# Narrow attention in a sixteen-stage kernel: other loads, other places for the bf16 splits, and the division by token

## The reference

```python
q, k, v = proj(Wq, bq), proj(Wk, bk), proj(Wv, bv)      # [b, 16, n, 8]
score = jax.nn.softmax(jnp.einsum('bhif,bhjf->bhij', q, k) / SCALE, axis=-1)   # SCALE = 128 / 19.5
attn = jnp.einsum('bhij,bhjf->bihf', score, v)
o = attn.reshape(b, n, f) @ Wo.T + bo
x = x + o
```

## Time and profile before

| | |
|---|---|
| median of 3 executions | 3803.88 us (3800.67, 3803.88, 3805.98) |
| the profiled execution | 3797.76 us, span of its profile 3796.1 us, 33099 instructions |
| TensorE busy | 2777.9 us (73%) |
| VectorE busy | 1910.9 us (50%) |
| ScalarE busy | 1454.2 us (38%) |
| GpSimd busy | 563.0 us (15%) |
| mean granted TensorE clock | 0.872 |
| L0b, first and second trip | 270.1 to 467.4, 2155.0 to 2351.7 us |
| L2b, first and second trip | 1168.5 to 1343.3, 3053.0 to 3227.5 us |

### The profile page before, as it was taken

The page is one execution under the profiler, slowest core; times in us unless marked ns, Lnnn a source line. Parts: engine busy times, 40 slices in busy tenths (PEclk is TensorE's granted clock), DMA queues, the critical chain, the costliest instruction groups (busy, mean ns, idle before and its releaser), DMA issues. The chain is left out here.

```text
span 3796.1 us, 33099 instructions
## 1 busy us (share of the span) xinstructions
PE 2777.9 (73%) x11584; PEld 1230.2 (32%) x11630; DVE 1910.9 (50%) x2675; ACT 1454.2 (38%) x2370; POOL 563.0 (15%) x376
## 2 busy tenths in 40 slices
PE   3565778999695797573846567889996957965647
PEld 1221164544342343131212212635443423422312
DVE  4858642554315613872549575425533166148635
ACT  2442412654242444432434334036542423434323
POOL 0532000000014010430006400000000140105300
PEclk8897969999797998895969889599997979988969
DMA  2001000000011110002000020000000011100010
GB/s 85 0 1 42 10 1 1 1 1 1 6 39 30 23 45 0 0 3 20 1 12 0 0 44 8 1 1 1 1 1 28 17 34 18 45 0 0 9 14 6
DMA packets 103312, 52.11 MB, mean 14 GB/s; under 512 B 75232, under 2 KB 91616, under 8 KB 103136
## 3 DMA queue, kind: packets, MB, share of 16 engines
q1 hardware_dynamic: 103136, 49.88, 5.6%
HBM read 40.02 MB, written 9.44 MB: 13 GB/s over the span
## 5 line engine op out<-in xcount | busy, mean ns | idle before, releaser
L1598 ACT ACTIVATE L1b_pr<-ps,L1b_mneg 128x512 f32<-128x512 f32 x256 | 173.5, 683 | 196.1 <-DVE L1b_mneg L1637 196.1
L518 POOL TENSOR_TENSOR xs<-xs,L2f_part 128x512 f32<-128x512 f32 x32 | 40.5, 1265 | 1286.6 <-DVE L2f_part L507 1286.6
L1635 DVE TENSOR_REDUCE L1b_m<-ps 128x2 f32<-128x1024 f32 x128 | 156.8, 1225 | 104.9 <-PE ps L1502 100.8
L1356 ACT ACTIVATE L0b_pt<-ps 128x1024 f32<-128x1024 f32 x128 | 129.5, 1023 | 208.6 <-PE ps L1294 206.7
L90 ACT ACT_TABLE_LOAD x32 | 41.1, 1283 | 423.3 <-PEq L671 180.5
L1403 DVE TENSOR_REDUCE L0b_mx<-ps 128x1 f32<-128x512 f32 x256 | 161.3, 685 | 46.8 <-PE ps L1278 38.9
L1046 POOL TENSOR_TENSOR L0a_db<-L0a_du,L0a_bs 128x1024 f32<-128x1024 f32 x64 | 150.3, 2353 | 224.4 <-ACT L0a_bs L1017 213.7
L1046 POOL TENSOR_TENSOR L3a_db<-L3a_du,L3a_bs 128x1024 f32<-128x1024 f32 x64 | 150.3, 2352 | 224.6 <-ACT L3a_bs L1017 214.1
L1356 ACT ACTIVATE L2b_pt<-ps 128x1024 f32<-128x1024 f32 (+3 forms) x128 | 88.5, 703 | 204.8 <-PE ps L1297 204.3
L1278 PE MATMUL ps<-L0b_ks,L0b_qs 128*128 128x512 bf16 x246 | 100.7, 446 | 87.8 <-DMA L0b_ks<-parts_dram 51.9
L1661 DVE COPY L1b_prt<-ps 128x512 f32<-128x512 f32 x128 | 88.6, 692 | 124.8 <-PE ps L1513 124.5
(11 more groups left out here) (567 smaller groups left out, 5787.8 us busy)
## 6 DMA issues: line engine op xcount, KB each, us to landing
L2f_w<-expert_dram SPq DMA_DIRECT2D x32, 256.0 KB, 3.0
L2g_w<-expert_dram SPq DMA_DIRECT2D x32, 256.0 KB, 3.1
weights<-w_dram SPq DMA_DIRECT2D x7, 789.5 KB, 8.8
parts_dram<-L0b_cut SPq DMA_DIRECT2D x4, 768.0 KB, 3.3
L0b_qs<-parts_dram SPq DMA_DIRECT2D x96, 32.0 KB
L0b_ks<-parts_dram SPq DMA_DIRECT2D x96, 32.0 KB
parts_dram<-L2b_cut SPq DMA_DIRECT2D x4, 768.0 KB, 3.3
L2b_qs<-parts_dram SPq DMA_DIRECT2D x96, 32.0 KB
```

The source lines that it names most:

```text
L1356: act.activation(pt[:, n % 3, 2 * half:2 * half + 2, q0:T], g.ps[:, 2 * (s % 2):2 * (s % 2) + 2, q0:T], ACT.Exp).then_inc(prob, 1)
L1598: act.activation(pr[:, s % 2, h, :], g.ps[:, 2 * (s % 2) + h, :], ACT.Exp, bias=mneg[:, s % 2, h:h + 1], accum_out=total[:, u % 2, t, h:h ...
L1635: dve.tensor_reduce(m[:, s % 2, :], g.ps[:, 2 * (s % 2):2 * (s % 2) + 2, :], AX.X, ALU.max).then_inc(max_raw, 1)
```

## The change

- `qs` and `ks` have 50 rows rather than 128, the tops' matmuls run over 48 of them and the scores' over 50; the fills are gone, and the two rows of ones in `ks` come by one DMA. The maxima are cut in two parts, not three.
- Heads of a unit lie next to each other, so that a DMA can load several units. Each part is sent as soon as it is cut; unit 0 is loaded first, then the other three of batch 1 in twelve DMAs, then all of batch 2 in twelve.
- Batch 1 is projected when its own norm is done. VectorE cuts batch 1, GpSimd batch 2. GpSimd also makes the three steps of the maxima.
- LEAD is 28.
- The division: TensorE transposes the copied sums (`turn`, slots 19, 35, 51 and after the last), VectorE takes the reciprocal of 32 denominators per row and multiplies 256 sums by them, TensorE transposes back (`turn_back`, slots 22, 38, 54 and after the last), ScalarE adds the bias.
- Batch 1's output matmul stands in slot 41, its addition in slot 42.

(Removed code that the functions above show is mostly left out here.)

```diff
-    STACK = 16 * 2 * len(Q_PART)
-    AHEAD = 2
-    LEAD = 25
+    LEAD = 28
     UN = NB * 4
+    SLOTS = 8 * UN
+    PARTS = 3
+    LOADS = 16 * 2 * len(Q_PART)
...
-        qs = st.sb("qs", [P, NB, 4, 4, T], BF16)
-        ks = st.sb("ks", [P, NB, 4, 4, T], BF16)
-        cut = st.sb("cut", [P, 3, 2, T], BF16)
...
+        qs = st.sb("qs", [ROWS + 2, NB, H, T], BF16)
+        ks = st.sb("ks", [ROWS + 2, NB, H, T], BF16)
+        cut = st.sb("cut", [P, NB, PARTS, 2, T], BF16)
...
-                def send_parts(b):
...
-                def stack(u):
+                sp.dma_start(ks[ROWS:ROWS + 2, :, :, :].rearrange("p b h (r c) -> p (b h r) c", c=P),
+                             bcast(g.cb[0:2, 544:544 + P], 1, NB * H * KT)).then_inc(ones_in, 16)
+                def send(b, part):
+                    if b == 0:
+                        sp.wait_ge(cut_dve, part + 1)
+                    else:
+                        sp.wait_ge(cut_pool, part + 1)
+                    sp.dma_start(g.parts_dram[b, :, part, :, :], cut[:, b, part, :, :]).then_inc(sent[part], 16)
+                def load(b, i0, n, part, landed):
+                    sp.wait_ge(sent[part], 16 * (b + 1))
+                    for x, table, dst in ((0, Q_PART, qs), (1, K_PART, ks)):
+                        for j in range(len(table)):
+                            if table[j] == part:
+                                src = g.parts_dram[b, 32 * i0:32 * (i0 + n), part, x, :].rearrange("(h f) t -> f h t", f=DH)
+                                sp.dma_start(dst[DH * j:DH * j + DH, b, 4 * i0:4 * (i0 + n), :], src).then_inc(landed, 16)
+                def send_max(u):
                     b, i = u // 4, u % 4
...
-                    sp.wait_ge(stacked, STACK * (u + 1))
...
-                for u in range(AHEAD):
...
+                    for p, ready in enumerate((m_hi, m_lo)):
+                        sp.wait_ge(ready, u + 1)
+                        sp.dma_start(qs[ROWS + p:ROWS + p + 1, b, 4 * i:4 * i + 4, :].rearrange("o r (t c) -> o (r t) c", c=P),
                                      mcut[:, u % 2, p, :]).then_inc(m_rows, 16)
...
-                    if u + AHEAD < UN:
-                        stack(u + AHEAD)
+                    sp.wait_ge(m_rows, 32 * (u + 1))
+                send(0, 0)
+                send(0, 1)
+                load(0, 0, 1, 0, unit0_in)
+                send(0, 2)
+                load(0, 0, 1, 1, unit0_in)
+                load(0, 0, 1, 2, unit0_in)
+                for part in range(PARTS):
+                    load(0, 1, 3, part, first_in)
+                send_max(0)
+                for part in range(PARTS):
+                    send(1, part)
+                for part in range(PARTS):
+                    load(1, 0, 4, part, second_in)
+                for u in range(1, UN):
+                    send_max(u)
...
-                    pe.wait_ge(ln.done, NB)
...
+                    pe.wait_ge(ln.done, b + 1)
+                    qb, kb, vb = ((0, 1, 2), (3, 6, 7))[b]
+                    pe.matmul(g.ps[:, qb, :], g.w(w + "_wq"), g.xn[:, b, :], start=True, stop=True)
+                    pe.matmul(g.ps[:, kb, :], g.w(w + "_wk"), g.xn[:, b, :], start=True, stop=True).then_inc(proj, 1)
...
-                    mm = pe.matmul(g.ps[:, 4 + a % 2, 0:span(t)], qs[:, b, i, r, t * P:(t + 1) * P], ks[:, b, i, r, 0:span(t)],
+                        if u == 0:
+                            pe.wait_ge(unit0_in, LOADS)
+                        elif b == 0:
+                            pe.wait_ge(first_in, LOADS)
+                        else:
+                            pe.wait_ge(second_in, LOADS)
+                    h, t = 4 * i + n // 4, n % 4
+                    mm = pe.matmul(g.ps[:, 4 + a % 2, 0:span(t)], qs[0:ROWS, b, h, t * P:(t + 1) * P], ks[0:ROWS, b, h, 0:span(t)],
                                    start=True, stop=not causal)
...
-                        mm = pe.matmul(g.ps[:, bank, q0:T], ks[:, b, i, r, kt * P:(kt + 1) * P], qs[:, b, i, r, q0:T],
+                        h, bank = 4 * i + 2 * half + x, 2 * (s % 2) + x
+                        mm = pe.matmul(g.ps[:, bank, q0:T], ks[:, b, h, kt * P:(kt + 1) * P], qs[:, b, h, q0:T],
...
-                        mm = pe.matmul(g.ps[32 * r:32 * r + 32, 6 + i // 2, q0:T], vpad[:, b, kt, 4 * r + i, :], pt[:, n % 3, r, q0:T],
+                        mm = pe.matmul(g.ps[32 * r:32 * r + 32, 6 + i // 2, q0:T], vpad[:, b, kt, 4 * i + r, :], pt[:, n % 3, r, q0:T],
...
-                def spread_den(c):
+                def turn(c):
                     pe.wait_ge(copied, c + 1)
...
+                    for t in range(KT):
+                        mm = pe.transpose(g.ps[:, 6 + c % 2, t * P:(t + 1) * P], acc[:, c % 2, t * P:(t + 1) * P], g.w("ident"))
+                    mm.then_inc(turned, 1)
+                def turn_back(c):
+                    pe.wait_ge(scaled, c + 1)
+                    for t in range(KT):
+                        mm = pe.transpose(g.ps[:, 6 + c % 2, t * P:(t + 1) * P], att[:, t, :, :].rearrange("p n x -> p (n x)"), g.w("ident"))
+                    mm.then_inc(back, 1)
+                def output(b):
+                    pe.wait_ge(at_ready, 2 * b + 2)
+                    for c in range(2):
+                        mm = pe.matmul(g.ps[:, 7, :], g.w(w + "_wo", c * P, P), at(2 * b + c), start=(c == 0), stop=(c == 1))
+                    mm.then_inc(out_ready, 1)
...
-                        spread_den(s // 16 - 1)
+                    if s % 16 == 3 and s > 16:
+                        turn(s // 16 - 1)
+                    if s % 16 == 6 and s > 16:
+                        turn_back(s // 16 - 1)
+                    if s == 41:
+                        output(0)
                 products(4 * UN - 1)
-                spread_den(2 * NB - 1)
...
-                        mm = pe.matmul(g.ps[:, b, :], g.w(w + "_wo", c * P, P), acc(2 * b + c), start=(c == 0), stop=(c == 1))
...
+                turn(2 * NB - 1)
+                turn_back(2 * NB - 1)
+                output(NB - 1)
...
+                def take_at(c):
+                    act.wait_ge(back, c + 1)
+                    act.wait_ge(cut_pool, PARTS)
+                    act.wait_ge(vpad_ready, 2 * NB)
+                    act.activation(at(c), g.ps[:, 6 + c % 2, :], ACT.Identity, bias=g.w(w + "_bv", c % 2, 1)).then_inc(at_ready, 1)
...
-                        pool.memset(dst[:, b, :, :, :], float(j)).then_inc(ones_in, 1)
...
+                pool.wait_ge(proj_in, 2 * NB)
+                for part in range(PARTS):
+                    pool.tensor_copy(cut[:, 1, part, :, :], val[1][:, :, :]).then_inc(cut_pool, 1)
+                    if part < PARTS - 1:
+                        pool.wait_ge(cut_pool, part + 1)
+                        pool.tensor_tensor(val[1][:, :, :], val[1][:, :, :], cut[:, 1, part, :, :], ALU.subtract).then_inc(rest_pool, 1)
+                        pool.wait_ge(rest_pool, part + 1)
+                for u in range(UN):
+                    pool.wait_ge(top_in, 17 * u + 17)
+                    if u >= 2:
+                        pool.wait_ge(m_rows, 32 * (u - 1))
+                    pool.tensor_copy(mcut[:, u % 2, 0, :], mt[:, u % 2, :]).then_inc(m_hi, 1)
+                    pool.wait_ge(m_hi, u + 1)
+                    pool.tensor_tensor(mt[:, u % 2, :], mt[:, u % 2, :], mcut[:, u % 2, 0, :], ALU.subtract).then_inc(m_rest, 1)
+                    pool.wait_ge(m_rest, u + 1)
+                    pool.tensor_copy(mcut[:, u % 2, 1, :], mt[:, u % 2, :]).then_inc(m_lo, 1)
...
+                def take(b):
+                    dve.wait_ge(proj, 2 * b + 1)
+                    dve.wait_ge(ln.done, NB)
+                    qb, kb = ((0, 1), (3, 6))[b]
+                    dve.tensor_scalar(val[b][:, 0, :], g.ps[:, qb, :], g.w(w + "_bq"), scale, ALU.add, ALU.mult).then_inc(proj_in, 1)
+                    dve.tensor_scalar(val[b][:, 1, :], g.ps[:, kb, :], g.w(w + "_bk"), None, ALU.add).then_inc(proj_in, 1)
+                take(0)
+                dve.wait_ge(proj_in, 2)
+                for part in range(PARTS):
+                    dve.tensor_copy(cut[:, 0, part, :, :], val[0][:, :, :]).then_inc(cut_dve, 1)
+                    if part < PARTS - 1:
+                        dve.wait_ge(cut_dve, part + 1)
+                        dve.tensor_tensor(val[0][:, :, :], val[0][:, :, :], cut[:, 0, part, :, :], ALU.subtract).then_inc(rest_dve, 1)
+                        dve.wait_ge(rest_dve, part + 1)
+                take(1)
...
-                    dve.tensor_copy(mcut[:, u % 2, 2, :], mt[:, 1, :]).then_inc(m_steps, 2)
...
-                def normalise(c):
...
+                        dve.wait_ge(m_lo, u - 1)
+                    dve.tensor_scalar(mt[:, u % 2, :], g.ps[0:16, 4 + a % 2, 0:P], -1.0, None, ALU.mult).then_inc(top_in, 1)
+                def divide(c):
+                    rows = g.ps[:, 6 + c % 2, :].rearrange("p (t n x) -> p t n x", n=8, x=16)
```

(36 more changed lines are left out.)

127 lines of the change are left out of this document (28 added, 99 removed).

## The result

The changed kernel takes 3970.24 us (median of 4, 3967.01 to 3979.68), against 3802.45 us of the kernel before (3800.67 to 3805.98): ratio 1.0446, 95% interval 1.043 to 1.0462. It is 168 us slower; I had forecast 3717 us. The sign is that of rival 3 (3853 us), and even that was too small.

The account below looks back on a forecast made before the run. No single engine bound it: casts and sends set the preparation, the VectorE-TensorE-VectorE loop the slots. Start -18.5, lead +0.7, periods -13.3, end -2.3, four stages -133: 3671 us; clock +46: 3717, range 3655 to 3792.

Parts of the forecast that it names:

- rival 3: Clock stays at 1.2 GHz to the end of the slots in L0b and L2b: +182, 3853 us, slower; chance 11%.
- Clock, +46: Slots of L0b and L2b: few rows hold TensorE at 1.2 GHz at first, +17 and +6 us, twice each.
- The first turn, behind slot 19: Slots: the first dense 128-row work, expected to end the 1.2 GHz stretch; 10 slow pairs of slots in L0b.
- Start, -18.5: Preparation of each stage: earlier projections, faster casts, split sends bring the first top sooner; -18.5 us, bounds -15 to -20.
- The loads of the other three units: nothing: Start: loads of units 1 to 3, about 8 us more, come before unit 1's tops want them; no cost.
- the lead: Tops ahead of the slots: three more tops, less five small steps off VectorE; +0.7 us per stage on 18.0.
- Behind GpSimd's waits only SP waits: Start: GpSimd's cut of batch 2 and maxima steps delay only SP; nothing lost while the rows' slack stands.
- Periods, -13.3: Slots, per stage: 6.6 us from six periods, 8.4 from two divisions, less 1.7 for the output matmul.
- the place of the transpose: Slots: with 28 tops ahead it falls where VectorE has caught up; 1.1 us a period (0 to 1.4).
- their removal alone may give nothing: Slots: five small steps per unit, 1.4 us, leave VectorE, but TensorE filled that time with scores and products anyway.
- End, -2.3: End of each stage, last copy to last addition: cheaper division cuts 10.4 us to about 8.1.
- The sum without the clock: Whole kernel: start, lead, periods and end, -33.4 us per stage, -133 in four stages, giving 3671 against the median.

Follow-up runs that it names:

- full_by_unit: full_unit1_first with batch 2 sent ahead of the first maxima, loaded unit by unit, and its keys filled on ScalarE: 3663.78 us, ratio 0.9638.
- change_full_rows: The changed kernel with 128-row operands again in tops and scores, regions filled ahead of their loads on GpSimd and ScalarE: 3739.72 us, ratio 0.982.
- change_masks_few_rows: The changed kernel with L2b's causal mask matmuls also on 48 or 50 rows, leaving part of the mask out: 3902.78 us, ratio 1.0255.
- before_few_rows: The kernel before with tops on 48 rows and scores on 51, fills and all else kept: 4090.31 us, ratio 1.0754.
- full_unit1_first: change_full_rows with unit 1's loads put ahead of those of units 2 and 3: 3732.63 us, ratio 0.9822.
- by_unit_lead_25: full_by_unit with LEAD back at 25 instead of 28: 3682.05 us, ratio 0.968.
- before_tops_few_rows: The kernel before with only the tops on 48 rows, scores and products on 128: 3886.26 us, ratio 1.0234.
- change_kick: The changed kernel, few rows kept, with two dense 128-row f32 matmuls put in ahead of slot 0: 3987.42 us, ratio 1.0485.

## Why the prediction was wrong

**The step that failed is "Clock, +46".** By the medians the 3970 us are the 3664 of full_by_unit, 76 for the loads and fills as change_full_rows has them (3740), and 230 for few rows, 67 of which change_masks_few_rows gives back. The forecast was 3671, nothing and 46. The mechanism of the 46 is shown by before_few_rows and change_full_rows: with few rows TensorE stays at 1.2 GHz. What is not separated is whether the number of rows does it or the changes between numbers of rows, since the slots with few rows have both; with 64 changes a unit fewer L2b stayed at 0.50 for most of its slots. The size is wrong in two places.

First, its end. "The first turn, behind slot 19" did not raise the clock. In L0b it rose at 421.6 us, behind the second turn (slot 35), and in the second trip at 2415.0, in the output matmul of slot 41; in L2b it stayed low nearly to the end of the slots, but for those 10 us of the second trip. I had chosen one length of low clock for four stages and gave its going on 11%. The stretch of L1a that I went by could have warned me: it is not all 32-row matmuls. Between them stand 2.7 us of matmuls with 128 rows, and they do not raise its clock either:

```profile
534.44 5.95 PE L723 MATMUL ps<-L1a_q,L1a_km 32*128 32x128 f32 x32
540.32 0.80 PE L737 MATMUL ps<-L1a_q,L1a_state 128*128 128x128 f32 x2
541.04 1.94 PE L740 MATMUL ps<-L1a_at,L1a_vpad 128*32 128x128 f32 x32
```

These are TensorE's lines ahead of the rise in L0b, in the two trips:

```profile
418.01 1.11 PE L1329 MATMUL ps<-weights,L0b_ln_xc 128*128 128x128 f32 x4
...
2410.97 3.78 PE L1343 MATMUL ps<-L0b_ln_sq,weights 128*128 128x512 f32 x4
```

Second, its price. A unit at the low clock costs 22.4 - 14.2 = 8.2 us in L0b, where I had 4 x 1.7 = 6.8, and 24.8 - 11.9 = 12.9 us in L2b, where I had 16.2 - 11.4 = 4.8. Of L2b's 12.9, 6.0 are the exposed loads (change_masks_few_rows) and 2.1 stay open; the prediction has no term for the loads, and no row that it read could show one, since every matmul of those stages had 128 rows. Rival 3 has the same hole: it gives L2b +40, and before_few_rows shows +88 (and +52 for L0b, where rival 3 gives +51).

**Start, -18.5:** from the stage's first instruction to the first top are 19.4 us against 40.3, so -20.9, beyond my bound of -20; the first top came 2.3 us after the last issue, not 4.0.

**"The loads of the other three units: nothing"** failed as well: I gave them 8 us more by their size, they landed 15 us after their last issue, and VectorE waited 5.8 us. So the lead was 25.0 us and not 18.7. Splitting them alone wins 11 us of the whole on the changed kernel and 7 with full rows, since the next wait stands behind them.

**"Behind GpSimd's waits only SP waits"** was the wrong question. What mattered is what is in transfer ahead of unit 1's rows: batch 2's twelve loads. Once the slots ran at full speed this cost 9 us (15 in full_unit1_first) and the clock besides; between full_unit1_first and full_by_unit lie 69 us.

**Periods, -13.3:** from the second to the last transposed maximum L0b takes 87.9 us in full_by_unit, against 101.5 in the earlier trace rows: -13.6. In L2b 73.6 against 84.7: -11.1. Inside it, in L0b, the place of the transpose is 1.05 us a period (I took 1.1, but in L2b it is nothing); the new division costs 14.70 - 14.20 = 0.5 us (I kept 0.8), the old one 4.9 to 5.0 more; the output matmul 16.41 - 14.70 = 1.7, as priced. Of the small steps I wrote that "their removal alone may give nothing", and with the old place it gave nothing: 15.25 us in by_unit_lead_25, 15.26 before. In the new place three of them on VectorE cost 0.78 us a period. So the two gains don't add: with either one missing, most of the 1.06 us of both is gone. **End, -2.3:** from the last copy to the end of the last addition are 8.0 us in full_by_unit, against 10.4 before and 8.1 forecast.

VectorE's lines of the new division (the first in L2b of the changed kernel) are 0.35 and 0.42 us, where I had 0.34 and 0.4:

```profile
1292.49 0.35 DVE L1468 RECIPROCAL L2b_inv<-ps 128x32 f32<-128x32 f32 x1
...
1292.87 0.42 DVE L1473 TENSOR_TENSOR xn<-ps,L2b_inv 128x256 f32<-128x256 f32 x1
```

**The sum without the clock** was 3671 us; full_by_unit, with full rows and the loads in order, has 3664. It is not the kernel that was priced, and some of the agreement is luck: the start and the division won more than I gave them, the place of the transpose in L2b less. As a sum, what is neither rows nor loads was right to 7 us.

In L0b of the changed kernel TensorE was busy 103.66 of 107.91 us at 0.50. The rule of the Trainium skill (the page "TensorE: Matmul & The Clock Gate", Part 1, What's actually happening) that the gate follows how busy the engine is does not fit this.

## What to carry to other kernels

Operand rows that add nothing to the result are not waste when they keep TensorE's clock up. Before cutting a matmul from 128 rows to 48, count what all of its work costs at 1.2 GHz, and fill the rows on an engine that is idle instead. Don't alternate matmuls of different row counts. Price a long wait of TensorE at more than its length, since the clock can fall in it. When loads are grouped, write out what is still in transfer ahead of each small one, at the new speed of the loop.

## What was not expected of the hardware

- A change of row count between two matmuls exposes the weight load: 0.11 us at 1.2 GHz, and at 2.4 GHz 1.4 us for 32 changes in before_tops_few_rows.
- In change_kick the same push over 128 rows, 3.7 us long, once left the clock at 0.50, followed by slots in which TensorE was busy 98% of the time, and three times raised it for only about 3.5 us.
- Twelve loads of 128 KB kept the DMA engines at a busy share of 0.56 and 58 to 64 GB/s for some 20 us, and TensorE had the 4 KB rows issued behind them only 16 us later (change_full_rows).
- GpSimd casts 128x1024 from float32 to bf16 in 1.05 us (I had 2), and ScalarE fills 128x8192 bf16 in 7.0 us, as long as GpSimd.
